# A convolution stage written out pair by pair: taps on VectorE alone, normalisations on ScalarE

## What is computed

```python
x = x + _L0_attn_a_ref(_layernorm(x, axis=-1), ...)
# in _L0_attn_a_ref; conv1: 128 groups, 1 -> 4 channels each, 5 taps; conv2: 128 groups, 4 -> 1, 5 taps
h = x.transpose(0, 2, 1)
h = gelu(conv1d_grouped(h, conv1_w, conv1_b, c))
h = conv1d_grouped(h, conv2_w, conv2_b, c)
h = h.transpose(0, 2, 1)
h = layernorm(h + x, ln0_g, ln0_b)
```

## Time and profile before

| | us |
|---|---|
| median of three runs | 2520.23 |
| lowest, highest | 2516.82, 2524.69 |
| the profiled execution, its time | 2517.0 |
| its span, first to last instruction | 2515.2 |
| busy in it: PE, PEld | 1968.9, 1370.5 |
| busy in it: DVE, ACT, POOL | 1470.1, 1140.1, 1198.3 |

### The profile page before, as it was taken

One profiled execution on the slowest core, in us unless ns is written; L12 is line 12 of the kernel. 1 busy time (PEld: TensorE's weight loads), 2 busy tenths in 40 slices (PEclk: granted clock), 3 DMA queues, 4 the chain that ended last, 5 costly groups with the idle time before them and its releaser, 6 DMA issues. The chain is left out here.

```text
span 2515.2 us, 44374 instructions
## 1 busy us (share of the span) xinstructions
PE 1968.9 (78%) x14950; PEld 1370.5 (54%) x14950; DVE 1470.1 (58%) x4240; ACT 1140.1 (45%) x2591; POOL 1198.3 (48%) x2018
## 2 busy tenths in 40 slices
PE   7885999988684787878588887899427888879991
PEld 6774888877441333334245544788403444338881
DVE  5997888884672344357476774433227767734232
ACT  2333555554342556634155554444204666555440
POOL 3553555552345555524555648244363544451434
PEclk9997999999885878888699988999757877679996
DMA  7000000000000000000000001567300000026672
GB/s 244 1 0 1 1 1 1 1 1 1 1 0 0 1 1 1 1 1 0 0 2 2 2 2 33 148 198 216 111 11 1 1 1 1 9 69 180 193 217 83
DMA packets 93935, 109.41 MB, mean 43 GB/s; under 512 B 12944, under 2 KB 76832, under 8 KB 93600
## 3 DMA queue, kind: packets, MB, share of 16 engines
q1 hardware_dynamic: 85536, 89.96, 12.2%
q0 software_dynamic: 8192, 16.79, 2.3%
HBM read 78.14 MB, written 28.57 MB: 42 GB/s over the span
## 5 line engine op out<-in xcount | busy, mean ns | idle before, releaser
L1491 DVE TENSOR_REDUCE a2mx<-PS 128x4 f32<-128x1024 f32 x128 | 155.9, 1218 | 64.1 <-PE PS L1672 63.5
L1927 ACT ACTIVATE a2prob<-PS 128x512 f32<-128x512 f32 x256 | 145.1, 600 | 97.8 <-PE PS L1696 97.7
L1491 DVE TENSOR_REDUCE a1mx<-PS 128x6 f32<-128x768 f32 x128 | 122.1, 954 | 75.2 <-PE PS L1679 74.9
L295 PE MATMUL PS<-cv_rT,cv_diag 128*128 128x256 f32 x640 | 150.5, 397 | 4.8 <-ACT cv_rT L343 4.8
L1930 ACT ACTIVATE a0prob<-PS 128x1024 f32<-128x1024 f32 x128 | 127.1, 1027 | 50.2 <-PE PS L1696 49.9
L1927 ACT ACTIVATE a1prob<-PS 128x384 f32<-128x384 f32 x256 | 114.1, 496 | 76.1 <-PE PS L1696 76.0
L1336 POOL TENSOR_SCALAR_AFFINE_SELECT a1prob<-a1prob 128x256 f32<-128x256 f32 x256 | 97.3, 409 | 98.3 <-ACT a1prob L1927 97.0
L295 PEld LDWEIGHTS PS<-cv_rT,cv_diag 128*128 128x128 f32 x640 | 127.3, 201 | 24.8 <-ACT cv_rT L343 4.2
L255 DVE SCALAR_TENSOR_TENSOR cv_y<-cv_gl,k_conv_w,cv_y 128x256 f32<-128x256 f32 x224 | 117.9, 598 | 0.0
L2411 DVE TENSOR_SCALAR m1bhid<-PS,m1bwr 128x256 f32<-128x256 f32 x92 | 40.3, 479 | 129.6 <-PE PS L2502 129.6
L2411 DVE TENSOR_SCALAR m1ahid<-PS,m1awr 128x256 f32<-128x256 f32 x92 | 40.3, 479 | 124.7 <-PE PS L2502 121.6
(11 more groups left out here) (529 smaller groups left out, 5624.0 us busy)
## 6 DMA issues: line engine op xcount, KB each, us to landing
m1awr<-in_wtab SPq DMA_DIRECT2D x46, 514.0 KB, 3.8
m1bwr<-in_wtab SPq DMA_DIRECT2D x46, 514.0 KB, 3.9
rows_in<-cv_blank SPq DMA_DIRECT2D x46, 128.0 KB, 2.3
m1axin<-rows_in SPq DMA_DIRECT2D x46, 128.0 KB
rows_out<-m1ayo SPq DMA_DIRECT2D x46, 128.0 KB, 1.9
m1bxin<-rows_in SPq DMA_DIRECT2D x46, 128.0 KB
rows_out<-m1byo SPq DMA_DIRECT2D x46, 128.0 KB, 2.0
X<-in_x SPq DMA_DIRECT2D x4, 512.0 KB, 6.3
```

Source lines behind the costliest of these rows:

```text
L295: last = pe.matmul(bank_c[u][:, j, :], lhsT=diag[:, j * TAPS + k, :], rhs=rT[:, par, u, k:k + N], start=(k == 0), stop=(k == TAPS - 1))
L1491: v.tensor_reduce(mx[:, 2 * j:2 * j + 2, :], MB[:, :, 0:SEG * seg_len].rearrange("p h (s n) -> p h s n", n=seg_len), AX.X, ALU.max).then_i ...
L1927: act.activation(prob[:, h % RING, 0:n_prob], SB[(b * NH + h) % NSB][:, 0:n_prob], ACT.Exp, scale=scale).then_inc(s["exp"], 1)
```

## The change

The loop is gone: every engine's stream is written out over i from -3 or -2 to 8, with `there(i)` for what exists. What runs at step i:

- DVE: all 20 taps of each sample of pair i, in the order of taps and samples in turn (for pair 0 sample by sample); after 12 of these 40, the statistics of X of pair i + 3; after 28, the statistics of y of pair i - 1. The diagonals are made after the statistics of pair 0, and PE waits for them four groups apart.
- ACT: copies, a new `first_y` (`rT` plus the bias, into `y`, which starts the sum), and both normalisations, as an activation with scale `rstd` and bias `shift`. Gelus count `gl` one by one; conv1 counts `c1` in two halves.
- POOL: only the roots, now four operations a sample (epsilon, negated mean, power, product), and smaller memsets.
- PE: conv1 of pair i + 1 for sample 0, `turn_y` of pair i - 1, `turn_r` of pair i + 2, conv1 for sample 1, `turn_back` of pair i - 1.

`y` is doubled, `z` and `wg` are gone. The diff, cut to its core:

```diff
@@ gpsimd @@
-            def conv2_last(i, par):
...
+            def root1(i):
+                for u in range(U):
+                    at = i * U + u
+                    pool.wait_ge(s["mv1"], at + 1)
+                    pool.tensor_tensor(ve[:, 0, u, :], mv[:, 0, u, :, 1], eps[:, 0, :], ALU.add).then_inc(s["ve1"], 1)
+                    pool.tensor_tensor(nm[:, 0, u, :], mv[:, 0, u, :, 0], minus[:, :], ALU.mult).then_inc(s["nm1"], 1)
+                    pool.wait_ge(s["ve1"], at + 1)
+                    finished(pool, s["out1"], at - U)
+                    pool.tensor_tensor(rstd[:, 0, u, :], ve[:, 0, u, :], half[:, :], ALU.pow).then_inc(s["rstd1"], 1)
+                    pool.wait_ge(s["nm1"], at + 1)
+                    pool.wait_ge(s["rstd1"], at + 1)
+                    pool.tensor_tensor(shift[:, 0, u, :], nm[:, 0, u, :], rstd[:, 0, u, :], ALU.mult)\
+                        .then_inc(s["shift1"], 1)
...
+            for i in range(-3, steps + 1):
+                if there(i + 3):
+                    root1(i + 3)
+                if there(i - 1):
+                    root2(i - 1)
@@ vector @@
+            def stats2(i):
+                for u in range(U):
+                    v.wait_ge(s["yt"], i * U + u + 1)
+                    finished(v, s["mv2"], (i - 1) * U + u)
+                    for h in range(NT):
+                        last = v.bn_stats(st[:, 1, u, h, :], bank_y[u][:, h * C:(h + 1) * C])
+                    last.then_inc(s["stats2"], 1)
...
+            def tap(i, t, u):
+                if t == 0:
+                    v.wait_ge(s["y0"], i * U + u + 1)
+                else:
+                    v.wait_ge(s[("tap0", "tap1")[u]], i * taps + t)
+                if t % TAPS == 0:
+                    v.wait_ge(s["gl"], (i * U + u) * MULT + t // TAPS + 1)
+                src = gl[:, i % 2, u, t // TAPS, t % TAPS:t % TAPS + N]
+                v.scalar_tensor_tensor(out=y[:, i % 2, u, :], in0=src, scalar=g["conv2_w"][:, t:t + 1],
+                                       in1=y[:, i % 2, u, :], op0=ALU.mult, op1=ALU.add)\
+                 .then_inc(s[("tap0", "tap1")[u]], 1)
+
             v.wait_ge(s["x_first"], 16)
+            for i in range(-3, steps + 1):
+                order = [(t, u) for t in range(taps) for u in range(U)] if i else [(t, u) for u in range(U) for t in range(taps)]
+                for at, (t, u) in enumerate(order):
+                    if at == 12 and there(i + 3):
+                        if i == -1:
+                            v.wait_ge(s["x_rest"], 48)
+                        stats1(i + 3)
+                    if at == 28 and there(i - 1):
+                        stats2(i - 1)
+                    if there(i):
+                        tap(i, t, u)
+                if i == -3:
+                    diagonals()
@@ tensor @@
+            for i in range(-2, steps + 1):
+                if there(i + 1):
+                    conv1(i + 1, 0)
+                if there(i - 1):
+                    turn_y(i - 1)
+                if there(i + 2):
+                    turn_r(i + 2)
+                if there(i + 1):
+                    conv1(i + 1, 1)
+                if there(i - 1):
                     turn_back(i - 1)
@@ scalar @@
+            def normed2(i):
+                for u in range(U):
+                    finished(act, s["unt"], (i - 1) * U + u)
+                    act.wait_ge(s["shift2"], i * U + u + 1)
+                    for h in range(NT):
+                        last = act.activation(r[:, 1, u, h, :], bank_y[u][:, h * C:(h + 1) * C], ACT.Identity,
+                                              bias=shift[:, 1, u, h:h + 1], scale=rstd[:, 1, u, h:h + 1])
+                    last.then_inc(s["out2"], 1)
...
+            def first_y(i):
+                for u in range(U):
+                    act.wait_ge(s["w"], 16 * len(g["first_loads"]))
+                    act.wait_ge(s["rT"], i * U + u + 1)
+                    finished(act, s["yt"], (i - 2) * U + u)
+                    act.activation(y[:, i % 2, u, :], rT[:, i % 2, u, PAD:PAD + N], ACT.Identity,
+                                   bias=g["conv2_b"][:, 0:1]).then_inc(s["y0"], 1)
+
+            def hidden(i, u):
+                act.wait_ge(s["zero"], 8)
+                finished(act, s[("tap0", "tap1")[u]], (i - 1) * taps - 1)
                 for j in range(MULT):
...
+                    if j % 2 == 0:
+                        act.wait_ge(s["c1"], (i * U + u) * 2 + j // 2 + 1)
+                    act.activation(gl[:, i % 2, u, j, PAD:PAD + N], bank_c[u][:, j, :], ACT.Gelu,
+                                   bias=g["conv1_b"][:, j:j + 1]).then_inc(s["gl"], 1)
...
-            def weigh_last(i, par, u):
...
+            for i in range(-3, steps + 1):
+                if there(i + 1):
+                    hidden(i + 1, 0)
+                if there(i + 2):
+                    take_r(i + 2)
+                if there(i + 1):
+                    first_y(i + 1)
+                if there(i + 3):
+                    normed1(i + 3)
+                if there(i - 1):
+                    normed2(i - 1)
+                if there(i + 1):
+                    hidden(i + 1, 1)
+                if there(i - 1):
                     save(i - 1)
```

More of the change, by code:

```diff
@@ L100, in conv_phase @@
     taps = MULT * TAPS
[L101 removed]
     with ExitStack() as ctx:
[L103 to L104 removed]
+        s = semaphores(nc, ctx, "cv", "x_first x_rest w later blank rows diag zero c1 gl y0 tap0 tap1 rt rT yt unt h "
+                                      "stats1 mv1 ve1 nm1 rstd1 shift1 out1 stats2 mv2 ve2 nm2 rstd2 shift2 out2")
         def sb(name, shape, dt=F32):
@@ L177, in conv2_last @@
-            def conv2_last(i, par):
-                held(pool, s["tap"], i * (U * (VT + 1)) - 1, s["ptick"])
-                for t in range(VT, taps):
-                    for u in range(U):
-                        if t == VT:
-                            held(pool, s["wg"], i * U + u, s["ptick"])
-                        else:
-                            pool.wait_ge(s["ptap"], (i * TAPS + t - VT - 1) * U + u + 1)
-                        pool.tensor_tensor(z[:, u, :], rT[:, par, u, PAD:PAD + N] if t == VT else z[:, u, :],
-                                           wg[:, u, t - VT, :], ALU.add).then_inc(s["ptap"], 1)
@@ L206, in _, with diagonals @@
-            v.wait_ge(s["zero"], 5)
-            def norm_stats(i, m, src):
-                stats, mvs = (("stats", "mv"), ("stats2", "mv2"))[m]
+            def diagonals():
+                v.wait_ge(s["w"], 16 * len(g["first_loads"]))
+                for j in range(MULT):
+                    for t in range(j * TAPS, (j + 1) * TAPS):
+                        last = v.tensor_scalar(diag[:, t, :], ident[:, :], g["conv1_w"][:, t:t + 1], None, ALU.mult)
+                    last.then_inc(s["diag"], 1)
@@ L334, in _, with normed1 @@
             act.preload_act_table_set("gelu_and_others")
-            act.wait_ge(s["w"], 16 * len(g["first_loads"]))
-            act.wait_ge(s["zero"], 5)
-            hv = HT[:, :, :].rearrange("p (i u) n -> p i u n", u=U)
-            def take_r(i, par):
-                held(act, s["ptap"], (i - 1) * (TAPS * U) - 1, s["atick"])
+            act.wait_ge(s["x_first"], 16)
+            def normed1(i):
+                if i == 2:
+                    act.wait_ge(s["x_rest"], 48)
+                for u in range(U):
+                    finished(act, s["rt"], (i - 1) * U + u)
+                    act.wait_ge(s["shift1"], i * U + u + 1)
+                    for h in range(NT):
+                        last = act.activation(r[:, 0, u, h, :], xv[:, i, u, h, :], ACT.Identity,
+                                              bias=shift[:, 0, u, h:h + 1], scale=rstd[:, 0, u, h:h + 1])
+                    last.then_inc(s["out1"], 1)
@@ L353, in weigh_last @@
[L353 to L360 removed]
+                    finished(act, s["c1"], ((i - 2) * U + u) * 2 + 1)
@@ L381, in _ @@
-            take_r(0, 0)
-            for u in range(U):
-                hidden(0, 0, u)
-                weigh_last(0, 0, u)
-            take_r(1, 1)
-            rounds(act, step)
-            save(steps - 1)
+            for i in range(-3, steps + 1):
[12 more added lines that the diff above has]
+                if there(i - 1):
+                    save(i - 1)
```

193 lines of the change are left out of this document (56 added, 137 removed).

## The result

| | before | after |
|---|---|---|
| median, us | 2520.48 (4 runs) | **2475.77** (4 runs: 2483.51, 2473.70, 2477.75, 2473.78) |
| ratio, 95% interval | 1 | 0.9828 (0.9800 to 0.9855) |
| the profiled execution, its time | 2517.0 | 2483.51 |
| span | 2515.2 | 2481.8 |
| busy PE, DVE, ACT, POOL | 1968.9, 1470.1, 1140.1, 1198.3 | 1962.3, 1446.0, 1141.3, 1162.8 |

The forecast was 2487 (2478 to 2506). The direction came true, and the mechanism in the main; DVE with a wait on ACT's queue, and not PE, sets the pace. Between the two profiled executions the difference is 33.5 us, where 33.3 were forecast, but that agreement is partly luck: the stage gave 36.9 us, and the rest of the kernel gave 3.4 back in this execution.

A forecast was written before the change was run, and what follows sets the result against it. PE was to pace the stage at 18.6 us a pair, 19.2 with waits; 51 + 115.2 + 17.2 + 7.3 = 190.7 us instead of 224.0, so 2520.2 - 33.3 = 2487 us, range 2478 to 2506.

The forecast's parts named there:

- A tap costs 0.40 us without POOL's additions: DVE's taps in the convolution stage: 0.40 us each once POOL is silent, so 40 a pair take 16.0 us.
- DVE's work, 18.3 a pair: Convolution stage, steady pair: 16.0 us of taps plus 2.3 of statistics on DVE, 18.3 us.
- Pace of a pair 19.2 in the steady state: Convolution stage: PE's 18.6 us sets the pace, plus 0.6 for waits across engines, 19.2 us a pair.
- DVE begins pair 1 at about 51.: Start of the convolution stage: DVE starts pair 1's taps at about 51 us, with PE in that pair's last conv.
- 6 x 19.2.: Middle of the convolution stage: DVE's pairs 1 to 6 at 19.2 us each, 115.2 us.
- Pair 7, 17.2.: Last pair of the convolution stage: only one set of statistics, so 17.2 us on DVE.
- Tail, 7.3.: From the end of the sum to the next stage: 7.0 us today, 7.3 with POOL's extra operations.
- The path over ACT's queue, 17.4 us,: From a DVE step's start through statistics, POOL's root and ACT to the second sample's first gelu: 17.4 us, fitting by 1.3.
- The extra of 0.6 us: Steady pair: added to PE's 18.6 us for waits across engines, bounded by 0 and 2.0 us.
- Rival 3: POOL's small operations stretch DVE's taps beside them: 2.8 us a pair added, 21.1 instead of 19.2, total 2500; chance 0.07.
- the span outside it has no reason to move: Rest of the kernel outside `conv_phase`: no change expected, so the whole gain is the stage's 33.3 us.
- rival 1's bound of 2481: Convolution stage as computed, with extra 0 per pair and start -1: stage 185 us, median 2481; chance 0.70.

The follow-up runs named there:

- pauses: The changed kernel plus a one-column DVE memset behind every second tap that follows statistics; median 2485.73 us, ratio 0.9867, stage end 185.7.
- taps_only: The kernel before, its loop and order kept, with all 20 taps on DVE and none on POOL or ACT; 2630.27 us, ratio 0.9980, stage end 215.8.
- norm_dve: The changed kernel with the normalisations done by DVE again; median 2489.82 us, ratio 0.9871, stage end 196.6.
- same_pair_pauses: The changed kernel with y completed within its own pair and a memset after every second of the first 24 taps; 2490.35 us, ratio 0.9865, stage end 187.5.
- group A: The first four follow-up runs, on one chip, beside the kernel before, which took 2635.51 us there.
- delay_sweep: The changed kernel with i memsets on POOL ahead of the product of pair i; median 2486.9 us, ratio 0.9861, stage end 189.7.
- after_fourth: The changed kernel unedited, on a fourth chip; median 2480.63 us against 2515.57 before, ratio 0.9851, stage end 188.5.
- shift_on_act: The changed kernel with POOL's product formed by ACT in two activations a sample; median 2477.01 us, ratio 0.9851, stage end 186.0.
- gelu_first: The changed kernel with two of the second sample's four gelus ahead of ACT's normalisations; median 2635.7 us, ratio 1.0002, stage end 214.3.
- again: The changed kernel unedited, run once more; median 2611.05 us against 2635.51 before, ratio 0.9913, stage end 198.0.

## Why the prediction came out as it did

**What held.** A tap costs 0.40 us without POOL's additions: right (6.39 for sixteen). DVE's work, 18.3 a pair: 18.02. PE's, 18.6: 18.59, without a gap, at clock 1.00. ACT hidden, except by its order. The turn of y without a wait: right. Pace of a pair 19.2 in the steady state: 19.05, but by luck in its parts: 18.6 of PE and 0.6 were forecast, and it is 18.02 of DVE and a wait of 1.03.

**What the stage missed by, term by term.** 190.7 was forecast, 187.1 came.
- *DVE begins pair 1 at about 51.* It began at 48.2 (53.05, where 40 taps end, less 12 x 0.40). The step's own sum said 49.6; it was put at 51 by the place of PE and ACT, for which DVE did not have to wait, and the first tap came at 26.7, not 28. -2.8 us.
- *6 x 19.2.* Pair 7 was counted with one set of statistics, but pairs 5 and 6 have no statistics of X either, since these run three pairs ahead: two times 1.1 us too many. The rest is the pace and the wait for gelu, which came in five of the six pairs. 48.2 to 159.5 (154.71 + 12 x 0.40) are 111.3 instead of 115.2. -3.9 us.
- *Pair 7, 17.2.* It has the wait for gelu too: 159.5 to 177.5. +0.8 us.
- *Tail, 7.3.* 177.5 to 187.1 are 9.6, +2.3 us. Pair 7's turn of y is queued on PE behind `turn_back` of pair 6, which waits for ACT and that for POOL's root; with taps beside it, this lasted until 178.53. The turn starts at 179.07, 1.6 us behind the end of the taps; before the change it started 0.3 us ahead of it. That is the price of completing a pair within the next one, and I had not asked for it at the end.

**The path over ACT's queue, 17.4 us,** was mis-sized. I took POOL's root at 1.33 us a sample from the earlier trace rows, where DVE is not running taps. Beside taps the four operations take 0.48, 0.44, 0.94 and 0.54: 2.4 us from the first to the next sample's first (73.25 to 75.67). Twice that is 2.2 us more than I had, and the slack was 1.3: hence DVE's wait of 1.03 us. The extra of 0.6 us had been chosen between 0 and 2.0, not worked out from this path.

**Rival 3 was the right pair of engines in the wrong direction.** The Trainium skill, SBUF — State Buffer, "Who interferes with whom", says that such a pair of instructions contends. It does here, by `pauses`: the product takes 0.20 us with memsets between the taps and 0.54 without. But the taps do not pay (476 ns on average in after, as in the earlier trace rows); POOL does.

**The step that failed for the total** is the first sentence: "the span outside it has no reason to move". The sum put the rest of the kernel at nothing. Of the 11.2 us by which the median came out below 2487, the stage's own terms account for 3.6; the other 7.6 lie outside it, and they are what carried the median out of the range. In the two profiled executions the rest did move: -2.6 us in the linear stage, whose length goes with the clock at which it begins, and +6.1 behind it (1947.1 to 1953.2). Between the medians it must have moved by about -7.8 (44.7 less 36.9), if the stage gave the same there. The executions that make the median were not traced, so which stages gave this stays open. What the runs do show is the size: the part behind the linear stage took 1944.4 to 1961.3 us in fourteen traces with the same code in it. The range allowed for this only the 3 us from rival 1's bound of 2481 to 2478. The four comparisons that were made of before and after give differences of 44.7, 31.7, 34.9 and (with the product kept out) 24.5 us; 33.3 lies within the intervals of the second and the third. How much of the first one's 44.7 is this chip's and how much those four executions', is open: the one that was profiled was the slowest of them.

**Where the gain comes from.** The stage ends at 224.0 or 221.8 us before, at 215.8 in `taps_only`, at 196.6 in `norm_dve`, and at 187.0 to 188.5 in the changed kernel with its products short. The chips differ, so the steps are rough.
- Taps on DVE in place of POOL: 6 to 8 us of the stage, and no gain that could be measured in the median.
- Normalisations on ACT: 8 to 10.
- The 19 us between `taps_only` and `norm_dve` belong to what the second has and the first has not: completion in the next pair, y doubled, PE's order with the turn in the middle, the split semaphores, statistics three pairs ahead, the start. Some of it can be named: a pair falls from 22.92 to 20.48 us, and of the 2.4 us 1.5 are waits of DVE. Between 60 and 160 us DVE waits 6.6 us for root and turn in `taps_only`, and 0.6 in `norm_dve`. So the order may well be worth more with the normalisations on DVE than the 2 us of `same_pair_pauses`, which has them on ACT. No run changed it alone there, and the 19 us were not divided further.

## What to carry to other kernels

When small operations of POOL lie on a chain, take their duration from rows where DVE works beside them as it will, not from a quiet stretch; and when DVE is given a long run of two-input operations with nothing between, ask who else works in that time. A memset of one column between the taps cost nothing here and kept POOL's product at 0.20 us; moving the product to ACT is the other way. When a stage is a sum of equal pairs, write out which pair has what: the last ones are shorter, and the tail inherits the queue of the one before. A gain of 1.3% is small beside the scatter of the untouched 90% of the kernel, so end such a comparison at the stage's mark, and at the next stage's, which can give a part back.

## What the runs showed of the hardware that I had not expected

- **POOL's two-input product can be kept out beside DVE's taps until the run of taps ends**: up to 11.6 us for 128 x 2 elements, which take 0.20 alone. There are 32 products of 1.7 us or more, in six kernels on three chips: most pairs of the three kernels of group A that have the product, two in `norm_dve`, one each in `delay_sweep` and `after_fourth`. Every one of them ended 0.05 to 0.06 us after the last tap of a run. DVE is not slowed.
- **Memsets between the taps let it through at 0.20 us**, in all 22 products between 50 and 178 us of each of four kernels, on three chips. None of these kernels ran on group A's chip, so that pauses cure it there too is likely and not shown; the same holds for the product on ACT (`shift_on_act` and the two like it, where no power lasted over 0.95 us). Why the product above all, no run here shows. In `taps_only`, which has no product, a power lasted up to 1.54 us, against 0.87 in the kernel before.
- **Less work can make it worse**: removing a wait of DVE (`gelu_first`) lengthened the runs of taps, and with them the time for which the product was kept out, and cost 16 us of the stage against `again`.
- **Group A's chip ran this kernel 4.6% slower than the other groups'** (2635.5 against 2515.6 to 2523.1 for the kernel before), with a mean granted clock of 0.84 where the others have 0.85 to 0.86. It is not slower throughout: up to 1553.6 us `again` is behind `after` by little more than its convolution stage (13.9 us, 10.9 of them there). The last three stages take 313.6, 432.8 and 306.0 us in it, and 269.6, 403.8 and 268.9 in `after`. No run shows why.
